# Attention with a split product: the half product directly behind the scores in steps 0 and 1 of each head, the transposes of probabilities behind it

## The chip, the cores and the metric

One NeuronCore of a Trainium2 chip runs the whole kernel. The metric is the device time of one execution in microseconds, as the median of several runs of the same program.

## The reference, cut to what matters

Each of 8 batches has 512 tokens (rows of x) and 512 context rows. Queries, keys and values come from low-rank products; there are 16 heads of width 128 and a rotary part of width 64 that all keys share.

```python
kv_c = kv @ W_kvc ; q_c = layernorm(x) @ W_dq
scores = (q_nope @ k_nope.T + q_rope @ k_rope.T) * scale
scores = where(k_ids <= seg and k_ids >= seg - 8, scores, -1e30)
attn = softmax(scores)
out = concat_heads(attn @ v) @ W_o
x = x + out
y = layernorm(x)
x = x + (y + spline(layernorm(y)))   # token-wise, small tables
```

The inputs are float32. Only the order of the work inside the attention is touched by the change; what is computed stays the same.

## The kernel before, in words

The kernel is written engine by engine: each engine has its own program, in an order written out by hand, and the engines meet at semaphores. Lines are those of the profile.

**Split operands.** An operand of a matmul is kept as a high part, rounded by ACT, and a low part, the rest, computed by DVE from the same source bank (value minus high part). A product of two operands is three matmuls (high-high, high-low, low-high). A PSUM bank comes free only when DVE has made its low part, or has added it to its target.

**Loops.** For each batch b (8) there are four quads q of four heads i each. A head has four score tiles of 128 queries by 512 keys, qt = 0 to 3, and on PE the program of one head (`head`, from L2797) is four steps, one per tile. Step s begins with the scores of tile s (five matmuls of 128x512, L2613 to L2638, into psS0 or psS1). Then follow fillers:

- step 0: the turn of tile 2 of the head before; the half product; the queries of the next head (9 matmuls, L2589, psA)
- step 1: the turn of tile 3 of the head before; the half product; the keys of the next head (6 matmuls, L2598, psB)
- step 2: `attend` of the head before (12 matmuls, L2666, psD); the turn of tile 0; a half product
- step 3: the turn of tile 1; values or a half product

In head 1 of a quad, steps 0 and 1 also hold one block of values each (6 matmuls, L2609, psD), between turn and half product. At the end of head 0 two blocks of values run, the second into psC.
In quad 0 heads 1 to 3 have another order in steps 2 and 3 ("late"), and no half products, since these belong to the quad before.
Between quads, `rope_queries` (18 matmuls, L2580) stands ahead of head 3. In the last head of a batch, transposes of the next batch's input (`turn_stage`, L2524) stand where the queries would be.

**The turn** (`turn_probs`, L2640) is four 128x128 transposes of one tile of probabilities into psT (or psE for some tiles), L2653. It waits for the normalised tile and for the low part of the tile that was in the bank before:

```python
pe.wait_ge(s_prob, n + 1)
done = n - 1 if beside else n
if done > 0:
    pe.wait_ge(s_ptlo, done)
```

**The half product** (`product`, L2670) is six matmuls (L2684) of the quad before against a part of W_o, into psC in steps 0 and 2 and mostly psE in steps 1 and 3. It waits for the weights, for the low part of its left operand (`product_lo`, L1975 on DVE) and for its bank:

```python
pe.wait_ge(s_wo[n % 2], 16 * (n // 2 + 1))
pe.wait_ge(s_aplo, n + 1)
wait_free(free, pos_p(b, q, j, u))
```

Which half product runs where is told by `groups(b, q, i, step)` (L500). It gives nothing for quad 0, and for head 0 only steps 0 and 1.

**ACT's order** in a head: normalise tile 3 of the head before (L1513); high part of the turned tile 2 (L1521); exponents of tile 0 (L1507); values and the high part for a product where due; normalise tile 0; high part of the turned tile 3; `rope_hi` (L1503) in head 3 of quads 1 and 2; exponents of tile 1; later exponents of tile 2, high part of q and k of the next head (L1478, L1482), and so on.

**DVE's order** in a head: masked scores of tile 0 (L1948); low part of the turned tile 2 (L1960); reciprocal of the row sums of tile 0 (L1954); second half of the rotary work in head 3 of quads 1 and 2 (L1912 to L1917); the sum of the half product into acc (L1990, L1993); a piece of the token-wise part of the batch before; then the same for step 1 with the turned tile 3, `product_lo` (L1975), and so on. In step 3 come `q_lo` (L1921) and `k_lo` (L1926) of the next head, which the next scores wait for, then the low part of the turned tile 1 (L1960), the reciprocal and, in head 3, `product_lo` for the next head 0. At the end of head 0 stand two `values_lo` (L1933), the second of which frees psC.

POOL makes the low part of the rotary queries (L1104), which SP moves by DMA into `q_rope_stack` for the next quad.

Of the kernel before, what the change touches and what calls it, by code (L numbers as in the profile page):

```python
# [27 lines left out]
def xattn_ffn_kernel(nc, x, ctx_in, seg, w_kvc, w_dq, w_uq, w_qr, w_uk, w_kr, w_uv, w_o,  # L28
# [26 lines left out]
    def pos_a(b, q, k):  # L55
        if q == 0 and k == 0:
            return b * AN + 2
        return b * AN + A0 + q * AQ + k

    def pos_b(b, q, k):  # L60
        if q == 0 and k == 0:
            return b * BN + 1
        return b * BN + B0 + q * BQ + k
# [35 lines left out]
    def tile_no(b, q, i, qt):  # L99
        return b * H * TT + (q * HQ + i) * TT + qt  # L100
# [5 lines left out]
    with ExitStack() as ctx:  # L106
# [393 lines left out]
        def groups(b, q, i, step):  # L500
            if q == 0:
                return []
            if i == 0:
                return [(q - 1, 0, step)] if step < 2 else []
            if i == HQ - 1 and q == NQ - 1 and b < B - 1:
                return [[(q - 1, 5, 0)], [(q - 1, 5, 1)], [(q - 1, 6, 1)], [(q - 1, 6, 0)]][step]
            return [(q - 1, 2 * i - 1 + step // 2, step % 2)]
# [1987 lines left out]
        def _(pe):  # L2495
# [106 lines left out]
            def values(b, q, *kts):  # L2602
                pe.wait_ge(s_wuv, 16 * (b * NQ + q + 1))
                for kt in kts:
                    ps, full, free = values_bank(q, kt)
                    wait_free(free, pos_v(b, q, kt))
                    for c in range(CB):
                        for a, s in ((0, 0), (0, 1), (1, 0)):
                            mm_ = pe.matmul(ps[:, :], kvc[a][:, c, kt * P:(kt + 1) * P], wuv[:, s, c, :],  # L2609
                                            start=c + s + a == 0, stop=c == CB - 1 and a == 1)  # L2610
                    mm_.then_inc(full, 1)

            def scores(b, q, i, qt, very_first):  # L2613
                n = tile_no(b, q, i, qt)
                if qt == 0:
                    pe.wait_ge(freeA, pos_a(b, q, 1 + i) + 1)
                    pe.wait_ge(s_khi, b * H + q * HQ + i + 1)
                    pe.wait_ge(s_stack[i], 64 * (b * NQ + q + 1))
                    if i == 0 and q == 0:
                        pe.wait_ge(s_rhi, b * (NQ + 1) + 2)  # L2620
                if not (very_first and qt < 2):
                    pe.wait_ge(s_sm, n - 1)
                cols = slice(qt * P, (qt + 1) * P)
                ps = psS[qt % 2][:, :]
                pe.matmul(ps, qh[:, cols], kh[:, :], start=True, stop=False)  # L2625
                pe.matmul(ps, ql[:, cols], kh[:, :], start=False, stop=False)  # L2626
                if i == 0 and q == 0 and qt == 0:
                    pe.wait_ge(freeB, pos_b(b, q, 1 + i) + 1)
                    pe.matmul(ps, qh[:, cols], kl[:, :], start=False, stop=False)
                    pe.wait_ge(s_krlo, b + 1)  # L2630
                    pe.matmul(ps, stack[:, i, cols], krh[:, :], start=False, stop=False)
                    pe.matmul(ps, stack[:, i, cols], krl[:, :], start=False, stop=True).then_inc(s_S, 1)
                    return
                pe.matmul(ps, stack[:, i, cols], krh[:, :], start=False, stop=False)  # L2634
                pe.matmul(ps, stack[:, i, cols], krl[:, :], start=False, stop=False)  # L2635
                if qt == 0:
                    pe.wait_ge(freeB, pos_b(b, q, 1 + i) + 1)
                pe.matmul(ps, qh[:, cols], kl[:, :], start=False, stop=True).then_inc(s_S, 1)  # L2638
# [157 lines left out]
            def body(b, first, last):  # L2796
                def head(q, i, q0, nxt=None):  # L2797
                    head0 = q0 and i == 0
                    vf = first and head0
                    before = (q, i - 1) if i > 0 else (q - 1, HQ - 1)  # L2800

                    def out(step):
                        for o, j, u in groups(b, q, i, step):
                            product(b, o, j, u)

                    quad, j = (q, i + 1) if i < HQ - 1 else (nxt, 0)

                    values_first = i == 1 and q0
                    if values_first:
                        values(b, q, 2)  # L2810
                    scores(b, q, i, 0, vf)
                    if not head0:
                        turn_probs(b, *before, 2)
                    if i == 1 and not values_first:
                        values(b, q, 2)
                    out(0)
                    if quad is not None:
                        queries(b, quad, j)
                    elif not last:
                        turn_stage(b + 1, 0, False)  # L2820

                    scores(b, q, i, 1, vf)
                    if not head0:
                        turn_probs(b, *before, 3)
                    if i == 1:
                        values(b, q, 3)
                    out(1)
                    if quad is not None:
                        keys(b, quad, j)

                    scores(b, q, i, 2, vf)
                    late = q == 0 and i > 0
                    if head0:
                        values(b, 0, 0)
                    elif not late:
                        attend(b, *before)
                    if not late:
                        turn_probs(b, q, i, 0)
                    out(2)

                    scores(b, q, i, 3, vf)
                    if late:
                        attend(b, *before)
                        turn_probs(b, q, i, 0)
                    turn_probs(b, q, i, 1)
                    if i == 0 and not q0:
                        values(b, q, 0)
                    out(3)
                    if i == 0:
                        values(b, q, 1)  # L2850

                for i in range(HQ - 1):
                    head(0, i, True)
                for q in range(1, NQ):
                    rope_queries(b, q)
                    head(q - 1, HQ - 1, False, q)
                    for i in range(HQ - 1):
                        head(q, i, False)
                head(NQ - 1, HQ - 1, False)
                o = NQ - 1  # L2860
                if last:
                    out_proj(0)
                    turn_probs(b, o, HQ - 1, 2)
                    out_proj(1)
                    out_proj(2)
                    turn_probs(b, o, HQ - 1, 3)
                    for w in range(3, 2 * TT - 1):
                        out_proj(w)
                    attend(b, o, HQ - 1)
                    out_proj(2 * TT - 1)  # L2870
                    return
                turn_stage(b + 1, 1, False)
                turn_probs(b, o, HQ - 1, 2)
                turn_stage(b + 1, 2, False)
                turn_probs(b, o, HQ - 1, 3)
                product(b, o, 0, 0)
                attend(b, o, HQ - 1)
                product(b, o, 0, 1)
                product(b, o, 1, 0)
                turn_stage(b + 1, 3, False)  # L2880
                product(b, o, 1, 1)
                down_q(b + 1)
                product(b, o, 2, 0)
                product(b, o, 2, 1)
                turn_stage(b + 1, 0, True)
                turn_stage(b + 1, 1, True)
                product(b, o, 3, 0)
                product(b, o, 3, 1)
                rope_queries(b + 1, 0)
                turn_stage(b + 1, 2, True)  # L2890
                turn_stage(b + 1, 3, True)
                product(b, o, 4, 0)
                product(b, o, 4, 1)
                down_kv(b + 1)
                product(b, o, 5, 0)
                product(b, o, 5, 1)
                into_heads(b + 1)
                product(b, o, 6, 0)
                product(b, o, 6, 1)
# [198 lines left out]
```

## Time and profile before

| | |
|---|---|
| median of 3 runs | 3016.24 us (3015.66 to 3018.25) |
| the profiled execution | 3017.6 us, its span 3015.8 us |
| granted TensorE clock, mean | 0.983 |
| busy share | PE 97%, weight loads 79%, DVE 73%, ACT 54%, POOL 32% |
| DMA | 592.74 MB in 179312 packets, 197 GB/s on average |

The span runs from the first to the last instruction of the program. PE's matmuls are pipelined: the recorded length of one is longer than its share of the stream, so the time that a block of matmuls takes is read from the start of its first one to the start of the next block. "Idle before" is time in which the engine had nothing running, with the operation that ended the wait.

### The profile page before, as it was taken

What the parts mean: (1) busy time and instruction counts of PE and PEld (TensorE: products, weight loads), DVE (VectorE), ACT (ScalarE), POOL (GpSimd) and SP (SyncE); (2) the same over time, 40 slices, a digit from 0 to 9 for tenths busy, and PEclk for the clock granted to TensorE, in tenths of its full rate; (3) what the DMA queues carried; (4) which work ended last, traced back from release to release, by engine and by line L of the source; (5) the groups of instructions that cost most, each with busy time, mean ns of one, the idle gap of its engine ahead of it and who ended that gap; (6) DMA issues with size and microseconds to landing.
All of it is one profiled execution on the core that took longest, in us unless ns stands there. A gap on an engine that the chain in (4) does not pass through costs nothing.

```text
span 3015.8 us, 41488 instructions
## 1 busy us (share of the span) xinstructions
PE 2919.0 (97%) x13886; PEld 2369.3 (79%) x13886; DVE 2208.5 (73%) x4548; ACT 1638.6 (54%) x3220; POOL 951.0 (32%) x683
## 2 busy tenths in 40 slices
PE   8999999999999999999999999999999999999985
PEld 6777878887888878888888888888788887888862
DVE  4566768877577866778678876788757787677777
ACT  3666636555365545655465563655536554555553
POOL 6356572112422133211512214211242213321127
PEclk9999999999999999999999999999999999999985
DMA  7655776555755566555665556555474556655431
GB/s 244 219 195 197 261 280 206 192 178 177 271 177 183 169 229 241 184 186 174 253 209 185 179 187 253 205 192 189 175 271 172 187 167 225 232 191 180 144 99 4
DMA packets 179312, 592.74 MB, mean 197 GB/s; under 512 B 38416, under 2 KB 52368, under 8 KB 143648
## 3 DMA queue, kind: packets, MB, share of 16 engines
q1 hardware_dynamic: 174032, 589.22, 55.9%
q0 software_dynamic: 5072, 0.88, 0.7%
q8 instruction: 116, 1.90, 0.3%
q14 instruction: 92, 0.75, 0.1%
HBM read 471.31 MB, written 85.14 MB: 185 GB/s over the span
## 4 chain that ended last, share of the span: by engine, by line
PE 83%; DVE 6%; ACT 4%; issue 2%; POOL 2%; DMA 1%; SPq 0%; ACTq 0%; POOLq 0%; DVEq 0%
PE psD L2666 10%; PE psC L2684 9%; PE psA L2589 8%; PE psE L2684 7%; PE psT L2653 6%; PE psB L2598 6%; PE psD L2609 4%; PE psS L2625 3%; PE psS L2626 3%; PE psS L2638 3%; PE psS L2634 3%; PE psS L2635 3%; PE psA L2541 3%; PE psA L2580 2%; PE psB L2580 2%
## 5 line engine op out<-in xcount | busy, mean ns | idle before, releaser
L1507 ACT ACTIVATE exps_ring<-exps_ring,neg_max 128x512 f32<-128x512 f32 x512 | 371.1, 725 | 395.5 <-DVE neg_max L1948 394.6
L1521 ACT ACTIVATE probsT_hi<-psT 128x512 fp32r<-128x512 f32 x432 | 258.4, 598 | 383.4 <-PE psT L2653 380.1
L1948 DVE CUSTOM_DVE_ANT_0 exps_ring<-psS,mask 128x512 f32<-128x512 f32 x512 | 352.5, 689 | 144.7 <-PE psS L2638 128.9
L1960 DVE TENSOR_TENSOR probsT_lo<-psT,probsT_hi 128x512 fp32r<-128x512 f32 x432 | 298.4, 691 | 151.7 <-ACT probsT_hi L1521 143.5
L1513 ACT ACTIVATE exps_ring<-exps_ring,row_sum_inverse 128x512 f32<-128x512 f32 x512 | 368.5, 720 | 43.1 <-DVE row_sum_inverse L1954 43.0
L2684 PE MATMUL psC<-w_o_product,attn_product 128*128 128x512 f32 x1302 | 350.3, 404 | 6.4 <-POOL w_o_product L1133 2.9
L2653 PEld LDWEIGHTS psT<-ident,exps_ring 128*128 128x128 f32 x1728 | 208.5, 140 | 92.3 <-issue 46.6
L2653 PE MATMUL psT<-ident,exps_ring 128*128 128x128 f32 x1728 | 261.0, 273 | 18.2 <-DVE probsT_lo L1960 15.8
L2684 PEld LDWEIGHTS psC<-w_o_product,attn_product 128*128 128x128 f32 x1302 | 232.6, 189 | 55.6 <-issue 9.7
L2684 PE MATMUL psE<-w_o_product,attn_product 128*128 128x512 f32 x1008 | 272.4, 405 | 0.0
L2589 PE MATMUL psA<-q_c_hi,w_uq_ring 128*128 128x512 f32 x768 | 261.1, 394 | 0.0
L2625 PE MATMUL psS<-k_hi,q_hi 128*128 128x512 f32 x512 | 205.7, 402 | 5.7 <-DVE q_lo L1921 4.1
L2684 PEld LDWEIGHTS psE<-w_o_product,attn_product 128*128 128x128 f32 x1008 | 178.5, 189 | 31.8
L2666 PE MATMUL psD<-probsT_hi,values_hi 128*128 128x512 f32 x512 | 200.0, 391 | 0.6
L2626 PE MATMUL psS<-k_hi,q_lo 128*128 128x512 f32 x512 | 199.9, 390 | 0.0
L1954 DVE RECIPROCAL row_sum_inverse<-row_sum 128x1 f32<-128x1 f32 x512 | 83.4, 163 | 158.9 <-ACT exps_ring L1507 157.5
L2666 PE MATMUL psD<-probsT_hi,values_lo 128*128 128x512 f32 x512 | 199.6, 390 | 0.0
L2666 PE MATMUL psD<-probsT_lo,values_hi 128*128 128x512 f32 x512 | 199.2, 389 | 0.0
L2638 PE MATMUL psS<-k_lo,q_hi 128*128 128x512 f32 x504 | 197.5, 392 | 0.0
L2634 PE MATMUL psS<-k_rope_hi,q_rope_stack 128*128 128x512 f32 x504 | 197.1, 391 | 0.0
L2635 PE MATMUL psS<-k_rope_lo,q_rope_stack 128*128 128x512 f32 x504 | 196.7, 390 | 0.0
L2598 PE MATMUL psB<-kv_c_hi,w_uk_ring 128*128 128x512 f32 x512 | 181.0, 394 | 0.0
(492 smaller groups left out, 6588.3 us busy)
## 6 DMA issues: line engine op xcount, KB each, us to landing
w_o_product<-w_o_split SPq DMA_DIRECT2D x190, 1024.0 KB, 5.1
w_uq_ring<-w_uq_split SPq DMA_DIRECT2D x112, 384.0 KB, 5.4
w_o_split<-w_o_product SPq DMA_DIRECT2D x28, 1024.0 KB, 5.4
w_uk_ring<-w_uk_split SPq DMA_DIRECT2D x112, 256.0 KB, 3.0
w_uv_quad<-w_uv_split SPq DMA_DIRECT2D x28, 1024.0 KB, 7.0
w_qr_sorted<-w_qr_split SPq DMA_DIRECT2D x28, 768.0 KB, 4.3
x_stage<-in_x_dram SPq DMA_DIRECT2D x32, 512.0 KB, 5.2
x_stage<-in_ctx_dram SPq DMA_DIRECT2D x32, 512.0 KB, 6.1
```

Of the source, the lines that this page charges most:

```text
L1507: act.activation(E[:, qt, :], E[:, qt, :], ACT.Exp, scale=-1.0, bias=mx[:, i % 2, qt:qt + 1], accum_out=rs[:, i % 2, qt:qt + 1]).then_inc( ...
L1513: act.activation(E[:, qt, :], E[:, qt, :], ACT.Copy, scale=ri[:, i % 2, qt:qt + 1]).then_inc(s_prob, 1)
L1948: dve.tensor_tensor_reduce(E[:, qt, :], psS[qt % 2][:, :], mask[:, qt, :], -SCALE, BIG, ALU.add, ALU.min, mx[:, i % 2, qt:qt + 1]).then_in ...
L1960: dve.tensor_tensor(PT[1][:, :, qt * P:(qt + 1) * P], turn_bank(q, i, qt)[:, :].rearrange("p (c n) -> p c n", c=TT), hi.bitcast(F32), ALU. ...
L2589: mm_ = pe.matmul(psA[:, :], wuq[:, i % 2, s, c, :], qc[a][:, c, :], start=c + s + a == 0, stop=c == QB - 1 and s == 1)
L2598: mm_ = pe.matmul(psB[:, :], wuk[:, i % 2, s, c, :], kvc[a][:, c, :], start=c + s + a == 0, stop=c == CB - 1 and s == 1)
L2625: pe.matmul(ps, qh[:, cols], kh[:, :], start=True, stop=False)
L2626: pe.matmul(ps, ql[:, cols], kh[:, :], start=False, stop=False)
L2638: pe.matmul(ps, qh[:, cols], kl[:, :], start=False, stop=True).then_inc(s_S, 1)
L2653: mm_ = pe.transpose(ps[:, c * P:(c + 1) * P], E[:, qt, c * P:(c + 1) * P], ident)
L2666: mm_ = pe.matmul(psD[:, :], V[v][:, kt, i * P:(i + 1) * P], PT[p][:, kt, :], start=kt == 0 and v + p == 0, stop=kt == TT - 1 and v == 1)
L2684: mm_ = pe.matmul(ps[:, :], operand_part(n, a)[:, i, u, :], WO[:, n % 2, o, i, :], start=i + a + o == 0 and not goes_on, stop=i + a == 2, ...
```

## The change

In steps 0 and 1 of each head PE's program issues the half product, `out(0)` or `out(1)`, directly behind the scores. The turn of tile 2 or 3 of the head before, and in head 1 the block of values, come behind it. The programs of ACT, DVE, POOL and SP are not changed.

```diff
                     scores(b, q, i, 0, vf)
+                    out(0)
                     if not head0:
                         turn_probs(b, *before, 2)
                     if i == 1 and not values_first:
                         values(b, q, 2)
-                    out(0)
                     if quad is not None:
                         queries(b, quad, j)
                     elif not last:
                         turn_stage(b + 1, 0, False)
 
                     scores(b, q, i, 1, vf)
+                    out(1)
                     if not head0:
                         turn_probs(b, *before, 3)
                     if i == 1:
                         values(b, q, 3)
-                    out(1)
                     if quad is not None:
                         keys(b, quad, j)
```

## Rows read from the trace of the kernel before

**Rows 1.** The page: busy time and share by engine; the chain by engine.

```profile
PE 2919.0 (97%) x13886; PEld 2369.3 (79%) x13886; DVE 2208.5 (73%) x4548; ACT 1638.6 (54%) x3220; POOL 951.0 (32%) x683
...
PE 83%; DVE 6%; ACT 4%; issue 2%; POOL 2%; DMA 1%; SPq 0%; ACTq 0%; POOLq 0%; DVEq 0%
```

**Rows 2.** PE timeline, heads 3 and 0: start us, length, what, count.

```profile
1006.46 0.60 PE L2653 MATMUL psT<-ident,exps_ring 128*128 128x128 f32 x4
1006.82 1.64 PE L2684 MATMUL psC<-w_o_product,attn_product 128*128 128x512 f32 x6
1008.29 0.39 PE L2589 MATMUL psA<-q_c_hi,w_uq_ring 128*128 128x512 f32 x1
...
1023.33 0.40 PE L2625 MATMUL psS<-k_hi,q_hi 128*128 128x512 f32 x1
...
1024.70 0.63 PE L2653 MATMUL psT<-ident,exps_ring 128*128 128x128 f32 x4
1025.41 1.63 PE L2684 MATMUL psC<-w_o_product,attn_product 128*128 128x512 f32 x6
1026.87 0.39 PE L2589 MATMUL psA<-q_c_hi,w_uq_ring 128*128 128x512 f32 x1
```

**Rows 3.** PE timeline, steps 3 and 0 around the start of head 1.

```profile
1041.92 0.39 PE L2625 MATMUL psS<-k_hi,q_hi 128*128 128x512 f32 x1
...
1043.06 0.60 PE L2653 MATMUL psT<-ident,exps_ring 128*128 128x128 f32 x4
...
1044.88 1.54 PE L2684 MATMUL psC<-w_o_product,attn_product 128*128 128x512 f32 x6
1046.27 0.39 PE L2589 MATMUL psA<-q_c_hi,w_uq_ring 128*128 128x512 f32 x1
```

**Rows 4.** DVE timeline, end of head 0, then head 1 to head 2.

```profile
1042.75 0.69 DVE L1933 TENSOR_TENSOR values_lo<-psC,values_hi 128x512 fp32r<-128x512 f32 x1 [0.28 <-ACT values_hi L1488]
...
1055.46 0.69 DVE L1948 CUSTOM_DVE_ANT_0 exps_ring<-psS,mask 128x512 f32<-128x512 f32 x1 [0.28 <-PE psS L2638]
...
1059.12 0.69 DVE L1960 TENSOR_TENSOR probsT_lo<-psT,probsT_hi 128x512 fp32r<-128x512 f32 x1 [0.37 <-ACT probsT_hi L1521]
...
1060.32 0.68 DVE L1993 TENSOR_TENSOR acc<-acc,psC 128x512 f32<-128x512 f32 x1
1061.14 0.69 DVE L1948 CUSTOM_DVE_ANT_0 exps_ring<-psS,mask 128x512 f32<-128x512 f32 x1
...
1061.76 0.69 DVE L1921 TENSOR_TENSOR q_lo<-psA,q_hi 128x512 fp32r<-128x512 f32 x1
...
1063.19 0.69 DVE L1960 TENSOR_TENSOR probsT_lo<-psT,probsT_hi 128x512 fp32r<-128x512 f32 x1 [0.15 <-ACT probsT_hi L1521]
```

**Rows 5.** PE timeline: first turn in head 0 (quad 1), head 2, head 3 (quad 3).

```profile
865.60 0.63 PE L2653 MATMUL psT<-ident,exps_ring 128*128 128x128 f32 x4 [0.40 <-DVE probsT_lo L1960]
...
1062.68 0.40 PE L2625 MATMUL psS<-k_hi,q_hi 128*128 128x512 f32 x1
...
1064.03 0.63 PE L2653 MATMUL psT<-ident,exps_ring 128*128 128x128 f32 x4
...
1082.30 0.63 PE L2653 MATMUL psT<-ident,exps_ring 128*128 128x128 f32 x4
1083.01 1.62 PE L2684 MATMUL psC<-w_o_product,attn_product 128*128 128x512 f32 x6
```

**Rows 6.** DVE timeline, head 3 of quad 2 and start of head 0.

```profile
1014.38 0.16 DVE L1954 RECIPROCAL row_sum_inverse<-row_sum 128x1 f32<-128x1 f32 x1 [0.96 <-ACT exps_ring L1507]
...
1022.43 0.69 DVE L1921 TENSOR_TENSOR q_lo<-psA,q_hi 128x512 fp32r<-128x512 f32 x1
...
1024.63 0.67 DVE L1975 TENSOR_TENSOR attn_product<-attn_sum,attn_product 128x512 fp32r<-128x512 f32 x1
```

**Rows 7.** ACT timeline, step 1 of head 3 of quad 2.

```profile
1012.11 0.60 ACT L1521 ACTIVATE probsT_hi<-psT 128x512 fp32r<-128x512 f32 x1 [2.58 <-PE psT L2653]
...
1013.55 0.71 ACT L1507 ACTIVATE exps_ring<-exps_ring,neg_max 128x512 f32<-128x512 f32 x1
```

## The prediction

> **What bounds the kernel now.** The page comes first: PE is busy 97% of the span, DVE 73%, ACT 54%, and the chain that ended last is 83% PE [rows 1]. So a change pays only by taking idle time out of PE's queue, and costs by putting some in. PE works its queue in order, and so do ACT and DVE in this trace; none of the three overtakes its own waiting instruction. Then I read PE's timeline around the two edited steps, from start to start, because a recorded matmul is longer than its place in the stream. Without a wait the four turns take 0.36 us to the start of the product behind them, and that product takes 1.47 to the next block [rows 2]; behind ordinary matmuls a product takes 1.39 [rows 3]. So about 0.1 us belongs to the change from transposes to matmuls, whichever matmuls follow: a turn costs 0.47 in either order and a product 1.37. Moving them is neutral as long as nothing waits. All that counts is who waits.
>
> **What the change does.** It moves the half product of step 0 and of step 1 from behind the turn of the last head's tile 2 or 3 to directly behind the scores. On quad 0 there is no half product, so nothing changes there. On the other three quads it is 12 heads x 2 steps x 8 batches = 192 moves. In head 1 the product also passes six values matmuls: turn and values together take 1.82 there [rows 3], so these take 1.46. No instruction is added or removed, on any engine; SP and POOL keep their order. Each turn comes 1.37 us later against PE's own stream, each product 0.47 earlier (1.9 in head 1).
>
> **The gains.** In heads 0 and 2 the first turn waits for psT, which DVE frees by the low part of the last head's tile 1. In head 2 the low part ends at 1063.88 (1063.19 + 0.69) [rows 4] and the turn starts 0.15 later, at 1064.03; scores begun at 1062.68 would have let it start at 1063.81, as five score matmuls take 1.13 [rows 3, 5]. That is 0.21 lost, and the product now covers it: 21 heads in batches 1 to 7, 4.4 us. In head 0 of quad 1 PE idles 0.40 before that turn, and 0.15 more goes to the weight load behind the release [rows 5]: 0.55 x 7 = 3.9 us.
>
> **Term A, the product in heads whose operand is late.** In head 0 of quads 2 and 3 the product too starts late: the turn is at 1024.70, the product at 1025.41 and not 0.36 later [rows 2]. The row behind it is product_lo, which starts at 1024.63 and ends at 1025.30 [rows 6]. The product can't start earlier in the new order either; so the turn, which before fitted into its wait, now comes after it: 1.37 + 0.47 from 1025.41 is 1027.25 against 1026.87, 0.38 lost. Head 3 of the last quad shows the same gap (1082.30, 1083.01) [rows 5]. Three heads a batch, 21 x 0.38 = 8.0 us.
>
> **Term B, head 1.** Its product writes psC, last used by the values of tile 1 at the end of head 0. DVE frees psC at 1043.44 (1042.75 + 0.69) [rows 4], so the product could start at 1043.59. Before, the turn and one values block lay in between; now the product is due at 1043.06, when the scores end [rows 3]. The direct stall is 0.53. On top comes what DVE has fallen behind in head 0 (next term): between 0 and 1.37. I take 0.4, since DVE has several short idle stretches there, such as the 0.28 in that very row, which use up most of it. 0.9 x 21 = 18.9 us.
>
> **Term C, the late turn of tile 3 (step 1).** This is the main cost, and the trace of before hides it. ACT's queue is: high part of the turned tile 3, then exponents of tile 1. The high part starts as soon as the turn is done, after 2.58 idle, so it moves by 1.37, and the exponents behind it move too [rows 7]. DVE's reciprocal waits for those exponents (0.96 idle, released by them), and behind it on DVE stand, without slack of their own in head 3, product_lo, the adds, the masked scores of tiles 2 and 3, q_lo, and the next product_lo [rows 6]. Where DVE still idles in that stretch it waits for ACT, which has moved as well. In head 3 of quads 1 and 2, q_lo ends at 1023.12 (1022.43 + 0.69) [rows 6] and the scores that need it start at 1023.33 [rows 2]; with 0.15 for the release the slack is 0.06. So the next head starts 1.37 - 0.06 = 1.3 us late: 14 x 1.3 = 18.2 us. In head 1 the same 1.37 arrives with the second values block, but DVE idles 0.28 and 0.37 on the way and about 0.14 before the masked scores at 1061.14 (the add at 1060.32 ends by 1061.00); 0.58 is left, and q_lo, ending at 1062.45 for scores at 1062.68, has 0.08 of slack [rows 4, 5]. 0.5 x 21 = 10.5 us. In head 2, which has no work of the values on DVE, idle time of DVE should take it, and I cost it at nothing; if that cover went, it would be up to 1.3 more in each. Head 0's share is in term B. The attend of step 2 needs the same late tile; a block of keys and five score matmuls stand before it in most heads; in the last head of a batch the keys are missing, and I guess 0.5 there, which is in neither the sum nor its low bound.
>
> **What I cost at nothing.** POOL's sum for the rotary part and the transfer of q_rope_stack start 1.4 us later in head 3; three steps of scores, the attend and two products lie between them and their use. If that cover went, the price would be the same 1.3 already counted.
>
> **The sum.** Batches 1 to 7: -4.4 - 3.9 + 8.0 + 18.9 + 18.2 + 10.5 = +47.3 us. Batch 0 waits at other places (weights on their first way in) but has the same queues; I take it as one more such batch: 47.3 x 8/7 = +54 us. The profiled execution took 3017.6 us (its span is 3015.8), so 3071.6; it stood 1.4 above the median of the runs shown, so **3070 us**, slower by 1.8%.
>
> **Bounds.** Low: the direct effects only, with DVE and ACT soaking up the late turn: -4.4 - 3.9 + 8.0 + 21 x 0.53 = 10.8, x 8/7 = 12.4: 3028 us. High: head 1 gets all of the 1.37 (1.9 x 21 = 39.9), head 3 of the last quad loses 0.5 for its attend: 3.5: together 71.8, x 8/7 = 82: 3098 us.
>
> **Rivals.**
> 1. *Faster: the product fills the wait for psT.* Only the gains come true, and the late products and banks turn out free. Waits at the turn before: 0.21 x 21 in head 2, 0.55 x 7, and 0.2 in each of the 21 heads of term A: 12.5 us, x 8/7 = 14: 3002 us. For it: PE's stalls at the turn are there in the rows. Against it: the 0.35 between turn and product in head 0 has no other reader than product_lo. It decides at the product of head 1: if psC is free when the scores end, this rival is alive. The Trainium skill (Perfetto Trace Analysis, "Matmuls") says that independent matmul groups should rotate through PSUM banks, so that ACT and DVE empty one while the next group runs; by that rule the new order, in which a product stands between two users of psT, would be the better one and the sum would be this rival's. The rows on the low parts are against it here: what is emptied later is awaited later.
> 2. *Direct effects only*, 3028 us as worked out above: the queues of ACT and DVE catch up within each head. For it: DVE is busy only 73%. Against it: in head 3 the slack of q_lo is 0.06 us.
> 3. *Nothing measurable*: gains and losses cancel, about 3017 us. It needs term B to be zero and term C too.
> 4. *DVE becomes the bound*: each late start piles onto the next, 1.37 in every one of the 96 heads with products: +130 us, 3147. Against it: with 73% busy, DVE has idle time in every head on average [rows 1].
>
> **How the numbers follow.** What a measurement of this kernel can tell from no change is about 0.2%, 6 us. My forecast 0.70 (its own range 3050 to 3098), direct effects only 0.15, faster 0.07, nothing 0.05, DVE as the bound 0.03. The range of 3028 to 3098 takes in the forecast and rival 2. Slower by over 0.2%: 0.70 + 0.15 + 0.03 = 0.88; within: 0.05; faster: 0.07.
>
> **What would show it.** Right: in the changed kernel the first product of head 1 starts 0.5 to 1.4 us after the scores end, with DVE's values_lo as the releaser; the scores that open head 0 of quads 2 and 3 idle over 1 us for q_lo; the wait of the turns for probsT_lo is gone; PE's busy time is the same and its share falls to about 95%. Wrong: if those scores start without a wait, term C falls and the time goes to 3028; if ACT's exponents of tile 1 don't move against PE's scores, the whole chain argument is wrong.

## The result, and the profile after

The changed kernel takes 3080.34 us (median of 4 runs, 3079.46 to 3081.97), the kernel before 3016.76 us (4 runs, 3015.66 to 3018.25). The ratio is 1.0211, with a 95% interval of 1.0193 to 1.0229: 64 us slower, and clear of the noise. The forecast was 3070 us.

The page of the changed kernel, as in [rows 1]:

```profile
PE 2929.9 (95%) x13886; PEld 2367.0 (77%) x13886; DVE 2196.9 (71%) x4548; ACT 1636.3 (53%) x3220; POOL 948.7 (31%) x683
...
PE 68%; DVE 19%; ACT 6%; issue 4%; POOL 1%; DMA 1%; SPq 0%; ACTq 0%; POOLq 0%; DVEq 0%
```

PE's busy time is all but unchanged; its share falls from 97% to 95%, and no instruction has been added. In the chain of work that ended last DVE goes from 6% to 19%: PE's work is now broken by waits for DVE. The granted clock is the same (0.983 before, 0.982 after), so no time went there.

To see where the 64 us sit, I took from both traces the start of each head's four blocks of scores on PE and compared, step by step, the time from one block's start to the next. Differences in us; the sum is over batches 1 to 7, where the pattern repeats:

| place | each | count | sum | the forecast |
|---|---|---|---|---|
| head 0 of quad 1, step 0 | -0.58 | 7 | -4.1 | -3.9 |
| head 0 of quads 2, 3, step 0 | +0.33 | 14 | +4.6 | |
| last head of the batch, step 0 | +0.42 | 7 | +2.9 | these two: +8.0 |
| head 1, step 0 | +0.84 | 21 | +17.6 | +18.9 |
| head 3 of quads 1, 2, step 3 | +1.27 | 14 | +17.8 | +18.2 |
| head 1, step 3 | +0.48 | 21 | +10.0 | +10.5 |
| head 2, step 0 | -0.12 | 21 | -2.5 | -4.4 |
| last head of the batch, steps 1 to 3 | +1.1 | 7 | +7.7 | 0 |
| all of batches 1 to 7, with the small places not listed | | | +54.8 | +47.3 |
| batch 0 | | | +9.3 | +6.8 |

**Head 3 and the start of the next quad.** PE's timeline of the changed kernel, the place of [rows 2] (start, length, what, and in brackets the idle time before it):

```profile
1043.57 0.63 PE L2653 MATMUL psT<-ident,exps_ring 128*128 128x128 f32 x4 [1.08 <-DVE probsT_lo L1960]
...
1045.43 0.39 PE L2625 MATMUL psS<-k_hi,q_hi 128*128 128x512 f32 x1
...
1047.36 1.63 PE L2684 MATMUL psC<-w_o_product,attn_product 128*128 128x512 f32 x6 [0.62 <-issue]
1048.83 0.60 PE L2653 MATMUL psT<-ident,exps_ring 128*128 128x128 f32 x4
```

The turn of tile 1 in step 3 waits for 1.08 us of idle time, for the low part of tile 0. The scores follow at 1045.43 and the product, due 1.14 behind them, comes 0.8 late, 0.10 us behind the end of product_lo (1046.59 + 0.67). The turn, which stood in that gap before, now comes behind it.

**Why the low part is late.** ACT and DVE in the same head, the places of [rows 7] and [rows 6], and POOL's rotary sum:

```profile
1034.29 0.60 ACT L1521 ACTIVATE probsT_hi<-psT 128x512 fp32r<-128x512 f32 x1 [2.59 <-PE psT L2653]
1034.79 1.05 ACT L1503 ACTIVATE rope_hi<-rope_out 128x1024 fp32r<-128x1024 f32 x1
1035.74 0.71 ACT L1507 ACTIVATE exps_ring<-exps_ring,neg_max 128x512 f32<-128x512 f32 x1
```

```profile
1036.57 0.16 DVE L1954 RECIPROCAL row_sum_inverse<-row_sum 128x1 f32<-128x1 f32 x1 [0.95 <-ACT exps_ring L1507]
1036.65 2.21 DVE L1975 TENSOR_TENSOR attn_product<-attn,attn_product 128x512 fp32r<-128x512 f32 x1
...
1042.73 0.69 DVE L1960 TENSOR_TENSOR probsT_lo<-psT,probsT_hi 128x512 fp32r<-128x512 f32 x1 [0.32 <-ACT probsT_hi L1521]
...
1044.54 0.69 DVE L1921 TENSOR_TENSOR q_lo<-psA,q_hi 128x512 fp32r<-128x512 f32 x1
...
1046.59 0.67 DVE L1975 TENSOR_TENSOR attn_product<-attn_sum,attn_product 128x512 fp32r<-128x512 f32 x1
```

```profile
1035.92 2.40 POOL L1104 TENSOR_TENSOR rope_out<-rope_out,rope_hi 128x1024 f32<-128x1024 f32 x1 [12.47 <-ACT rope_hi L1503]
```

Head 3 starts at 1026.14 here and at 1005.33 before, 20.81 later. Taken off, the high part of tile 3 is at 1013.48 against 1012.11, the exponents at 1014.93 against 1013.55, the reciprocal at 1015.76 against 1014.38, q_lo at 1023.73 against 1022.43: the half product's 1.37 us, handed from queue to queue, with 1.30 left at q_lo.

Two paths lead from ACT's late high part to product_lo. One is the forecast's, by the exponents and the reciprocal. The other goes by `rope_hi`, which ACT has between the high part and the exponents, and POOL's rotary sum, which waits for it. The second one binds. The product_lo takes 2.21 us instead of its usual 0.67, and it ends 0.55 us behind the end of POOL's sum; in the kernel before it is the same, in all 16 heads 3 of quads 1 and 2:

```profile
1013.73 2.40 POOL L1104 TENSOR_TENSOR rope_out<-rope_out,rope_hi 128x1024 f32<-128x1024 f32 x1 [11.06 <-ACT rope_hi L1503]
```

```profile
1014.47 2.21 DVE L1975 TENSOR_TENSOR attn_product<-attn,attn_product 128x512 fp32r<-128x512 f32 x1
```

From the head's start, product_lo ends at 11.35 before and at 12.72 after. Without the sum beside it, it would have ended at about 11.2 in the changed kernel (1036.65 + 0.67 - 1026.14), no later than before: an estimate, by which the exponents' path alone would have cost nothing here. Both paths moved by the same 1.37, so this trace can't tell them apart by size. The step 0 kernel below does.

**Head 1 and head 2.** PE and DVE, the places of [rows 3], [rows 4] and [rows 5]:

```profile
1064.33 0.39 PE L2625 MATMUL psS<-k_hi,q_hi 128*128 128x512 f32 x1
...
1066.23 1.62 PE L2684 MATMUL psC<-w_o_product,attn_product 128*128 128x512 f32 x6 [0.61 <-DVE values_lo L1933]
1067.69 0.60 PE L2653 MATMUL psT<-ident,exps_ring 128*128 128x128 f32 x4
```

```profile
1065.40 0.68 DVE L1933 TENSOR_TENSOR values_lo<-psC,values_hi 128x512 fp32r<-128x512 f32 x1
```

```profile
1085.71 0.68 DVE L1921 TENSOR_TENSOR q_lo<-psA,q_hi 128x512 fp32r<-128x512 f32 x1
```

```profile
1086.44 0.50 PE L2625 MATMUL psS<-k_hi,q_hi 128*128 128x512 f32 x1 [0.30 <-DVE q_lo L1921]
...
1087.71 1.54 PE L2684 MATMUL psC<-w_o_product,attn_product 128*128 128x512 f32 x6
```

The product of head 1 is due at 1065.47 (scores at 1064.33 + 1.14) and starts at 1066.23, 0.15 behind the end of values_lo (1066.08): 0.76 late. The other 0.08 of this place is the product itself, which takes 1.46 to the next block instead of 1.37. The scores of head 2 wait for q_lo, and the first of them pays 0.13 more: five score matmuls take 1.27 from there instead of 1.14.

**The last head of a batch.** Its attend now waits, which it did not before:

```profile
1112.34 0.48 PE L2625 MATMUL psS<-k_hi,q_hi 128*128 128x512 f32 x1
...
1113.36 0.39 PE L2638 MATMUL psS<-k_lo,q_hi 128*128 128x512 f32 x1
1114.00 0.50 PE L2666 MATMUL psD<-probsT_hi,values_hi 128*128 128x512 f32 x1 [0.25 <-DVE probsT_lo L1960]
```

With the last score matmul at 1113.36 it was due 0.23 later, at 1113.59; it starts 0.41 behind that, when the low part of tile 3 is there. Most of the rest of the 0.68 that step 2 loses is its first matmul (0.34 instead of 0.22) and the scores, which take 0.11 longer directly behind a turn; that 0.11 is what step 1 has less.

### The profile page after: what moved, and what is told of

It is laid out like the page before. It is cut to its first block, busy times and chain, and to the rows that moved or that the text cites. A ratio compares the mean times of both kernels' runs of the same rounds, so it can differ in the third digit from the quotient of the medians.

```text
span 3080.2 us, 41488 instructions
## 1 busy us (share of the span) xinstructions
PE 2929.9 (95%) x13886; PEld 2367.0 (77%) x13886; DVE 2196.9 (71%) x4548; ACT 1636.3 (53%) x3220; POOL 948.7 (31%) x683
## 4 chain that ended last, share of the span: by engine, by line
PE 68%; DVE 19%; ACT 6%; issue 4%; POOL 1%; DMA 1%; SPq 0%; ACTq 0%; POOLq 0%; DVEq 0%
PE psA L2589 8%; PE psC L2684 8%; PE psE L2684 6%; PE psD L2666 5%; PE psT L2653 5%; PE psB L2598 3%; PE psD L2609 3%; PE psA L2541 3%; DVE probsT_lo L1960 3%; PE psS L2625 3%; DVE exps_ring L1948 3%; PE psS L2626 2%; PE psS L2634 2%; PE psS L2638 2%; PE psS L2635 2%
## 5 line engine op out<-in xcount | busy, mean ns | idle before, releaser
L2589 PE MATMUL psA<-q_c_hi,w_uq_ring 128*128 128x512 f32 x768 | 268.4, 404 | 0.0
L2684 PE MATMUL psE<-w_o_product,attn_product 128*128 128x512 f32 x1008 | 264.5, 398 | 0.0
```

The lines of the kernel that those rows point to most:

```text
L2589: mm_ = pe.matmul(psA[:, :], wuq[:, i % 2, s, c, :], qc[a][:, c, :], start=c + s + a == 0, stop=c == QB - 1 and s == 1)
L2684: mm_ = pe.matmul(ps[:, :], operand_part(n, a)[:, i, u, :], WO[:, n % 2, o, i, :], start=i + a + o == 0 and not goes_on, stop=i + a == 2, ...
```

## The experiments

Each kernel is the one before with the edit shown, on the same chip as the runs of the kernel before that it is compared with.

**Step 0 alone.** `out(0)` stands behind the scores, `out(1)` where it was:

```diff
                     scores(b, q, i, 0, vf)
+                    out(0)
                     if not head0:
                         turn_probs(b, *before, 2)
                     if i == 1 and not values_first:
                         values(b, q, 2)
-                    out(0)
```

> Only step 0 has the half product ahead of the turn; step 1 is as before. Queue theory (the late turn of tile 3 in step 1 holds ACT's exponents of tile 1 and with them DVE): terms A and B and the gains stay, term C goes, and the late turn of tile 2 in step 0 leaves some 0.4 us at the start of head 0 behind head 3: 3030 to 3042 us. Rival (the product's own waits for product_lo and values_lo in step 0 carry the whole loss): nearly all of the loss stays, 3070 us or more.

3034.11 us, ratio 1.0059 (1.0042 to 1.0075). The range of the queue theory holds it. PE's timeline in head 1:

```profile
1046.05 0.39 PE L2625 MATMUL psS<-k_hi,q_hi 128*128 128x512 f32 x1
...
1047.72 1.62 PE L2684 MATMUL psC<-w_o_product,attn_product 128*128 128x512 f32 x6 [0.38 <-DVE values_lo L1933]
1049.18 0.60 PE L2653 MATMUL psT<-ident,exps_ring 128*128 128x128 f32 x4
```

Head 1 loses 0.62 here. The product is due at 1047.19 and starts 0.53 later, the direct stall as forecast; the other 0.09 is the product's own, as above. DVE brings nothing from head 0: the low part that frees psC ends 1.52 behind the start of the head's scores, as before, against 1.73 with step 1 moved and 1.75 with both. So 0.23 of the 0.84 is DVE's lag, and it comes from step 1.

The start of head 0 behind head 3 loses only 0.14, where I had expected 0.4. POOL and DVE in head 3 of quad 2, which starts at 1009.00:

```profile
1017.63 2.40 POOL L1104 TENSOR_TENSOR rope_out<-rope_out,rope_hi 128x1024 f32<-128x1024 f32 x1 [11.32 <-ACT rope_hi L1503]
```

```profile
1018.55 0.16 DVE L1954 RECIPROCAL row_sum_inverse<-row_sum 128x1 f32<-128x1 f32 x1 [0.28 <-ACT exps_ring L1507]
1018.63 1.95 DVE L1975 TENSOR_TENSOR attn_product<-attn,attn_product 128x512 fp32r<-128x512 f32 x1
```

Against the kernel before, counted from the head's start, the reciprocal is 0.50 late and POOL's sum 0.23 (8.63 for 8.40); product_lo ends 0.23 late (11.58 for 11.35) and takes 1.95 instead of 2.21. It follows POOL's sum and not the reciprocal.

**Step 1 alone.** `out(1)` stands behind the scores, `out(0)` where it was:

```diff
                     scores(b, q, i, 1, vf)
+                    out(1)
                     if not head0:
                         turn_probs(b, *before, 3)
                     if i == 1:
                         values(b, q, 3)
-                    out(1)
```

> Only step 1 has the half product ahead of the turn; step 0 is as before. Queue theory: term C alone, 1.3 us at the start of head 0 in quads 2 and 3, 0.5 at the start of head 2, and the attend and the tail of the last head of a batch: 3050 to 3062 us. Rival: the product of step 1 waits for nothing in the changed kernel, so this one is within 3 us of the kernel before, 3017 us.

3052.85 us, ratio 1.0121 (1.0104 to 1.0138). So the larger part comes from the step in which the moved product itself waits for nothing; the rival is out. The wait is where the changed kernel has it, on another block, two steps later:

```profile
1030.83 0.63 PE L2653 MATMUL psT<-ident,exps_ring 128*128 128x128 f32 x4 [1.08 <-DVE probsT_lo L1960]
...
1032.69 0.39 PE L2625 MATMUL psS<-k_hi,q_hi 128*128 128x512 f32 x1
```

By place: 1.26 in head 3 of quads 1 and 2, 0.50 in step 3 of head 1, 1.1 in the last head. The two single kernels together lose 53 us, the change 64; 6.5 us of the difference are in batch 0 (9.3 against 1.1 + 1.7), whose waits for weights I have not taken apart. Most of the rest is in heads 1 and 2: step 0 of head 1 loses 0.84 with both and 0.62 + 0 alone, and step 0 of head 2 gains 0.12 with both, 0.22 and 0.09 alone.

**Step 1 alone, with the exponents ahead of the turned tile.** ACT and DVE change the order of two operations each:

```diff
                     normalise(b, q, i, 0)
+                    expo(b, q, i, 1)
                     if not head0:
                         turned(b, *before, 3)
                     if nxt is not None and q > 0:
                         rope_hi(b, nxt, True)
-                    expo(b, q, i, 1)
...
+                    invert(b, q, i, 1)
                     if not head0:
                         turned_lo(b, *before, 3)
-                    invert(b, q, i, 1)
```

> As the step 1 kernel, and in step 1 ACT makes the exponents of tile 1 ahead of the high part of the turned tile 3, and DVE the reciprocal ahead of its low part. Queue theory: the exponents and DVE's reciprocal no longer wait for the late turn, so the 1.3 us at head 0 goes; the 0.5 at head 2 comes through the values block of step 1 and stays: 3025 to 3038 us. Rival (the late turn costs through its bank or through the attend, not through what stands behind it on ACT): no gain on the step 1 kernel, 3050 us or more.

3037.27 us, ratio 1.0066 (1.0049 to 1.0083): 15.6 us less than without the swap. ACT, DVE, POOL and PE in head 3 of quad 2, which starts at 1012.95:

```profile
1020.30 0.72 ACT L1507 ACTIVATE exps_ring<-exps_ring,neg_max 128x512 f32<-128x512 f32 x1 [3.14 <-DVE neg_max L1948]
...
1021.09 0.60 ACT L1521 ACTIVATE probsT_hi<-psT 128x512 fp32r<-128x512 f32 x1
```

```profile
1021.15 0.16 DVE L1954 RECIPROCAL row_sum_inverse<-row_sum 128x1 f32<-128x1 f32 x1 [0.89 <-ACT exps_ring L1507]
...
1022.33 0.68 DVE L1975 TENSOR_TENSOR attn_product<-attn,attn_product 128x512 fp32r<-128x512 f32 x1
...
1023.68 1.64 DVE L2077 TENSOR_SCALAR candidates<-onehot 128x64 f32<-128x64 bf16 x1
...
1026.27 0.69 DVE L1948 CUSTOM_DVE_ANT_0 exps_ring<-psS,mask 128x512 f32<-128x512 f32 x1
```

```profile
1022.72 2.55 POOL L1104 TENSOR_TENSOR rope_out<-rope_out,rope_hi 128x1024 f32<-128x1024 f32 x1 [12.43 <-ACT rope_hi L1503]
```

```profile
1029.17 0.63 PE L2653 MATMUL psT<-ident,exps_ring 128*128 128x128 f32 x4
```

The exponents no longer wait for the late turn. The 1.26 at the start of the next quad is down to 0.07, and the 0.50 in head 1 is untouched, as expected. But the way there isn't the one expected. From the head's start the reciprocal is at 8.20, against 9.05 before and 10.43 in the changed kernel: 2.23 earlier than there. POOL's sum still comes as late as there, at 9.77. So product_lo now starts before the sum does and isn't held (0.68 instead of 2.21), and the sum holds another instruction instead: L2077, which takes 0.18 to 0.19 elsewhere in this trace, takes 1.64 and ends 0.05 behind POOL's sum, in all 14 heads 3 of quads 1 and 2 in batches 1 to 7. The masked scores behind it are at 13.32, against 13.14 before and 14.53 in the changed kernel. What the swap gains, 1.21 there, is the work that DVE now does ahead of the sum's end instead of behind it. No kernel moves the rotary work by itself, so POOL's part is read from the traces and not from an experiment of its own.

**The change without head 1.** In head 1 both steps keep the old order (`if i != 1` at the new place, the old place otherwise):

```diff
                     scores(b, q, i, 0, vf)
+                    if i != 1:
+                        out(0)
...
+                    if i == 1:
+                        out(0)
```

(the same for step 1)

> The change in all heads but head 1, which keeps the old order in both steps. Queue theory: the 0.84 us for values_lo in step 0 of head 1 and the 0.48 at the start of head 2 go, (0.84 + 0.48) x 21 = 28 us in batches 1 to 7 and some 3 in batch 0: 3050 us. Rival (DVE is the bound and what isn't lost in head 1 is lost in the next head): 3065 us or more.

3044.26 us, ratio 1.0091 (1.0074 to 1.0108), 6 us below the forecast of 3050. Both stalls of head 1 are gone and nothing takes their place in batches 1 to 7 (+23.9 there, where 54.8 - 17.6 - 10.0 = 27.2 was due; over half of the rest is head 2, which now gains its full 0.20). Batch 0 gives back 9.7 us rather than 3. The rival, DVE as the bound, is out.

**The change with the old step 1 in head 1.** As the change, but `out(1)` stands behind the values where i == 1:

```diff
                     scores(b, q, i, 1, vf)
+                    if i != 1:
+                        out(1)
...
+                    if i == 1:
+                        out(1)
```

> The change, but in step 1 of head 1 the turn, the values and the half product keep the old order (in step 0 they don't). Queue theory: the 0.48 us at the start of head 2 comes from the second block of values, which reaches DVE 1.37 us later behind the product; it goes, 21 x 0.48 = 10 us, and the 0.84 in step 0 of head 1 stays: 3068 to 3072 us. Rival (the 0.48 is what is left of the 0.84 of step 0, handed on by DVE): no gain, 3079 us.

3068.41 us, ratio 1.0171 (1.0156 to 1.0187), in the forecast range. The product of step 3 and the scores of head 2, with no wait between:

```profile
1075.95 1.65 PE L2684 MATMUL psE<-w_o_product,attn_product 128*128 128x512 f32 x6
1077.44 0.40 PE L2625 MATMUL psS<-k_hi,q_hi 128*128 128x512 f32 x1
```

In this trace step 3 of head 1 loses nothing and step 0 still 0.84. So the 0.48 comes through the second block of values, and the two stalls of head 1 are separate.

**The change without the last head of a batch.** Head 3 of quad 3 keeps the old order in both steps (condition `(q, i) != (NQ - 1, HQ - 1)` in the same form of edit).

> The change in all heads but the last one of a batch (head 3 of quad 3), which keeps the old order in both steps. Queue theory: there the new order costs 0.43 (product waits for product_lo) - 0.11 + 0.69 (attend waits for the low part of the late tile 3) + 0.67 (what stands behind it in the tail) = 1.7 us a batch, 12 us over batches 1 to 7 and some 3 in batch 0; all of it goes: 3063 to 3068 us. Rival (the tail of a batch is bound by DVE whatever PE's order is there): 3074 us or more.

3066.28 us, ratio 1.0163 (1.0147 to 1.0178), in the forecast range and 14 us less than the change. The tail of a batch was not bound by DVE before; the new order makes it so.

**Only where it gains.** The product is first in step 0 of head 2 and of head 0 of quad 1:

```diff
                     scores(b, q, i, 0, vf)
+                    if i == 2 or (q == 1 and i == 0):
+                        out(0)
```

> Only where the turn waits for its bank and the product's operands are early is the half product put first: step 0 of head 2, and step 0 of head 0 of quad 1; step 1 is as before. Queue theory: 0.22 x 21 + 0.57 x 7 = 8.6 us saved in batches 1 to 7 and under 1 in batch 0, nothing lost: 3006 to 3009 us. Rival (a turn that comes 1.4 us later always costs something behind it): 3012 us or more.

3007.93 us, ratio 0.9966 (0.9952 to 0.9979), in the forecast range. Head 2 of quad 3, the place of [rows 5]:

```profile
1059.96 0.39 PE L2625 MATMUL psS<-k_hi,q_hi 128*128 128x512 f32 x1
...
1061.12 1.53 PE L2684 MATMUL psC<-w_o_product,attn_product 128*128 128x512 f32 x6
1062.49 0.60 PE L2653 MATMUL psT<-ident,exps_ring 128*128 128x128 f32 x4
1062.84 0.48 PE L2589 MATMUL psA<-q_c_hi,w_uq_ring 128*128 128x512 f32 x1
```

From the scores to the queries it takes 2.88 us. Before, the product alone began 1.74 behind the scores there and the queries 1.47 later. Of the 0.33 between them 0.1 goes back in the queries, which start more slowly behind a turn. In this trace batches 1 to 7 save 8.8 us.

**The low part first.** The product is first in step 0 of heads 0 and 2 and of the last head. On DVE, product_lo is made ahead of the low part of the turned tile 1:

```diff
+                    if q > 0 and i == 2:
+                        product_lo(b, q - 1, 5)
+                    if i == HQ - 1 and q > 0 and not plain_quad(b, q):
+                        product_lo(b, q, 0)
                     if late:
                         turned_lo(b, q, i, 0)
                     turned_lo(b, q, i, 1)
...
-                    if q > 0 and i == 2:
-                        product_lo(b, q - 1, 5)
-                    if i == HQ - 1 and q > 0 and not plain_quad(b, q):
-                        product_lo(b, q, 0)
```

> The half product is first in step 0 of heads 0 and 2 and of the last head of quad 3, and on DVE the low part that it waits for (product_lo of parts 0 and 5) is made ahead of the low part of the turned tile 1; step 1 is as before. Queue theory: in head 0 of quads 2 and 3 and in the last head of the batch the product no longer waits and covers the turn's wait; there 0.57 us a head is saved instead of 0.33 to 0.43 lost, 21 x 0.57 = 12 us on top of the 8.6: 2995 to 2999 us. Rival (the low part of the turned tile 1 comes 0.6 later and the normalised tile 3 behind it, and the turn waits as much as before): 3005 us or more.

3009.35 us, ratio 0.9974 (0.9965 to 0.9983): a miss; the rival's range holds it, though not for its reason. Heads 0 of quads 2 and 3 turn from +0.33 into -0.53, as expected. The last head keeps losing (0.43 in step 0, 0.84 in step 3). DVE and POOL just ahead of it, and PE's product:

```profile
1075.32 1.69 DVE L1975 TENSOR_TENSOR attn_product<-attn,attn_product 128x512 fp32r<-128x512 f32 x1
```

```profile
1075.16 1.29 POOL L1149 TENSOR_TENSOR attn_sum<-attn 128x512 f32<-128x512 f32 x1 [5.34 <-issue]
```

```profile
1077.11 1.63 PE L2684 MATMUL psC<-w_o_product,attn_product 128*128 128x512 f32 x6 [0.76 <-issue]
```

Moved forward, product_lo of part 5 starts 0.16 us after POOL's sum and takes 1.69 instead of 0.67, so that the product waits as long as before. The 0.84 in step 3 I have not traced to a cause.

**The same with the swap of step 1.**

> As the low part first kernel, and in step 1 ACT makes the exponents of tile 1 ahead of the high part of the turned tile 3, DVE the reciprocal ahead of its low part. Queue theory: step 1's turn is not late here, so the swap has nothing to take away: within 3 us of the kernel without it. Rival (DVE's chain in head 3 sets the start of the next quad, and exponents made earlier shorten it): 4 us or more faster than without it.

3023.99 us, ratio 1.0021 (1.0011 to 1.0031). Both theories miss: the swap makes it 15 us slower. In its trace, against the kernel without the swap, the last head loses 0.65 more in step 2 and 0.3 more in step 3, and step 0 of head 1 loses 0.25. In step 2 of that head the trace shows how: the turn isn't late there, ACT's high part of tile 3 comes 1.1 us later behind the exponents, DVE's low part 1.1 later behind it, and the attend waits for that low part. For the other two places I take the same reason, not shown.

**The low part first, head 0 alone.** Only product_lo of part 0 is moved forward, and the product is first in step 0 of heads 0 and 2:

```diff
+                    if i == HQ - 1 and q > 0 and not plain_quad(b, q):
+                        product_lo(b, q, 0)
                     if late:
                         turned_lo(b, q, i, 0)
                     turned_lo(b, q, i, 1)
...
                     scores(b, q, i, 0, vf)
+                    if i in (0, 2):
+                        out(0)
```

> The half product is first in step 0 of heads 0 and 2 only, and DVE makes only product_lo of part 0 ahead of the low part of the turned tile 1; the last head of a batch, where the low part of part 5 took 1.69 instead of 0.67 us beside POOL's sum, is as before, and so is step 1. Queue theory: 3.9 + 4.4 + 14 x 0.53 = 15.7 us saved in batches 1 to 7, 1 to 2 in batch 0: 3000 to 3003 us. Rival (the 9 us lost in the last heads of the low part first kernel come from the early low part of head 3, not from that of head 2): 3007 us or more.

3003.00 us, ratio 0.9960 (0.9946 to 0.9974), at the upper end of the forecast range. It has the lowest median of all; against the kernel that moves only where it gains (0.9966) the intervals overlap, so it is faster than the kernels before and after, and not shown to be faster than that one. Start of head 0 of quad 3, DVE and PE:

```profile
1018.91 0.68 DVE L1975 TENSOR_TENSOR attn_product<-attn_sum,attn_product 128x512 fp32r<-128x512 f32 x1
```

```profile
1018.62 0.39 PE L2625 MATMUL psS<-k_hi,q_hi 128*128 128x512 f32 x1
...
1019.77 1.54 PE L2684 MATMUL psC<-w_o_product,attn_product 128*128 128x512 f32 x6
1021.15 0.60 PE L2653 MATMUL psT<-ident,exps_ring 128*128 128x128 f32 x4
1021.50 0.48 PE L2589 MATMUL psA<-q_c_hi,w_uq_ring 128*128 128x512 f32 x1
```

The product follows the scores at once. Part of the gain is given back at the end of the batch: there 0.6 us are lost in each of most batches, in the step behind the last scores. I have not looked for the reason.

## Why the prediction was right, point by point

- **What bounds it.** Right: no engine got more work, and the loss is PE's idle time.
- **The gains.** Head 0 of quad 1: right (0.58 for 0.55). Head 2: 0.21 forecast; in the kernel that moves only where it gains it is 0.18 to 0.22 by quad, in the changed kernel 0.12 is left, because the scores that open the head are themselves released late and the first takes 0.13 longer. That belongs to term C, whose price in head 1 is then 0.6 and not 0.5.
- **Term A.** Right in place and cause: 0.33 and 0.42 for 0.38. The kernels with the low part first remove it in head 0.
- **Term B.** Right: 0.84 for 0.9, released by values_lo as forecast; 0.53 of it direct, 0.23 brought by DVE (0.4 forecast), 0.08 in the product's own start. Taking head 1 out removes it.
- **Term C.** Right in its main point: the late turn of tile 3 holds back what stands behind its reader on ACT, and by that DVE. Step 1 alone shows it without terms A and B, and the swap on ACT takes it away in head 3. Right in size: 1.27 for 1.3, 0.48 for 0.5. Wrong in the link in head 3: product_lo had slack against the reciprocal, since it takes 2.21 us beside POOL's rotary sum and ends 0.55 behind it, before and after. The late turn reached DVE by `rope_hi` and that sum. The size came out all the same because both paths moved by the same 1.37; that is luck, and where they moved by different amounts, in the step 0 kernel, the expectation missed by it (0.14 for 0.4). Wrong in another detail: I had the scores of head 0 wait over 1 us for q_lo. They hardly wait, since the turn of tile 1 in step 3 has taken the delay one block earlier, for the low part of tile 0. The total is the same, as both stand on the same DVE chain.
- **What I cost at nothing.** Wrong in its reason: POOL's rotary sum was looked at only for its transfer, as something that costs nothing more than the 1.3 already counted. It is itself what passes the 1.3 on, by holding DVE.
- **What would show it.** That PE's turns would no longer wait for probsT_lo is wrong. The view of the turn's line gives idle time and number of waits, before and then after:

```profile
  DVE probsT_lo L1960: 15.8, 25
```

```profile
  DVE probsT_lo L1960: 28.9, 34
```

  The wait at the first turn of a head is gone; a larger one has come at the turn of tile 1.
- **The sum.** 54 us forecast, 64 measured. The term that was mis-sized is the last head of a batch: costed at nothing in the sum, with a guess of 0.5 for the attend in the upper bound. It takes 0.68 at the attend, and 0.7 in the step behind it in all batches but the last, less 0.17 in step 1 on average: 4.7 + 4.2 - 1.2, 7.7 us in seven batches. Leaving that head out gives 14 us back, step 0 and batch 0 included. Batch 0 is the other: 9.3 for 6.8.
- **The rivals.** Faster: its gains exist (the kernel with only them is 0.34% faster) but they need an operand or a bank that is free; where it isn't, they turn into losses. The Trainium skill's rule on rotating PSUM banks (Perfetto Trace Analysis, "Matmuls") pays where the emptying engine is in time, as in head 2 (0.21 gained), and doesn't where it isn't, as psC in head 1 shows (0.53 lost directly). Direct effects only: 3028 against 3080, out, since step 1 alone costs 36 us. DVE as the bound: out by the kernel without head 1.

## What to carry to other kernels

Before a block is moved back in a busy engine's queue, look at what stands behind its reader in the reader's own queue. Here four transposes that nobody on PE was waiting for came 1.37 us later, and the next quad started 1.27 us later, by way of ACT's rotary high part, POOL's sum behind it and a subtraction on DVE that had to wait for that sum. A wait of that last kind shows in no row as idle time, only as an instruction that takes over three times its length. And before one is moved forward, read the end of the operation that makes its operand or frees its bank: a wait that another block used to cover is paid in full once that block stands behind it. The same move gained in the heads where neither was so, so it is decided place by place and not once for a loop.

## What the runs showed of the hardware

A subtraction on DVE with both operands in SBUF (product_lo) took 0.67 to 0.69 us by itself, 1.69 when it started 0.16 us after a POOL sum of 1.29, and 2.21 beside POOL's rotary sum of 2.40, in the kernel before as in the changed one. In each of these cases it ended 0.55 us behind the end of POOL's sum. I had not expected that moving it by a few tenths of a microsecond would cost a whole one. The low part of a turned tile, with one operand in PSUM, took 0.67 to 0.69 wherever it stood.

The Trainium skill (SBUF — State Buffer, "Who interferes with whom") says that a DVE instruction with two SBUF inputs contends with a GpSimd instruction that reads SBUF, and that one with at most one SBUF input doesn't, outside the modes in which DVE takes both ports. The trace of the low part first kernel agrees: the sum ends at 1076.45, the subtraction at 1077.01, nearly its own length later. In the kernel with the swap an instruction with one SBUF input (L2077, a tensor_scalar on bf16) was held as well, 1.64 us instead of 0.18; the trace doesn't say in which mode it ran.
